# An adaLN block with attention and a router of two experts: the weight search by quarters of the partitions, and four moves at its edges

## The chip, the cores and the metric

One NeuronCore of a Trainium2 chip runs the whole kernel; the metric is the device time in microseconds of that core. The engines are TensorE (PE, matmul, with PEld for its weight loads), VectorE (DVE), ScalarE (ACT), GpSimd (POOL) and SyncE (SP, which here only issues transfers).

## The reference, cut to what matters

Input `x` is 8 batches of 256 tokens by 128 features.

```
mod = silu(c) @ wmod -> sa, ca, ga, sb, cb, gb      (ga, gb kept at least 0.25 in size)
h = layernorm(x) * (1 + ca) + sa
x = x + ga * attention(h)       16 heads of 8, ALiBi slopes, causal softmax, W_o
h = layernorm(x) * (1 + cb) + sb
x = x + gb * ffn(h)
ffn: probs = softmax(layernorm(h) * gamma + beta) @ Wr + br over 8 experts
     y_e = gelu(h @ W1_e + b1_e) @ W2_e + b2_e;   out = sum_e probs_e * y_e
     expert 0 has the weights as given; experts 1 to 7 all share one altered copy:
     thr_bot, thr_top = the 3276th smallest and the 3276th largest |w| of the matrix
     w -> 0.2 w where |w| >= thr_top;   1.8 w where |w| <= thr_bot
```

b1 and b2 are altered likewise. So only two experts are computed, plain and altered, the second with the sum of seven probabilities. For W1 and W2 (65,536 numbers each) the two thresholds have to be found exactly.

## The kernel before, in words

**The search.** The four thresholds (top and bottom of W1 and of W2) are found bit by bit, 31 bits, each from a count of how many |w| lie below a candidate. W1's absolute values lie in `wa` on partitions 0 to 63 and W2's on 64 to 127, 1,024 columns each. The candidate tile `cand` has a column for the top threshold and one for the bottom, so each bit needs two passes over `wa`: `sign_count(n, TOP, 1024)` on ACT, then `sign_count(n, BOT, 512)` on ACT beside `dve_counts(n)` (L1203, the other 512 columns) on DVE. In the five steps of `BY_ACT` ACT takes all 1,024 columns of both. `total(n)` (L936, L938) sums over partitions with two tiny matmuls into `psX`, `decide(n)` (L1208) compares, `next_cand(n)` (L1214) sets the next candidate. Bits 0 and 1 come ahead of the main loop, then one a step in steps 0 to 30 but 23 and 27.

**The loop.** Each engine has its program written out by hand; semaphores alone tie them. Steps t = 0 to 39: each of the first 32 takes four heads of one batch through scores (`s_unit`, L767 first), row maxima (`maxima`, L1224, L1228, DVE), with a lag of five steps the exponentials (`e_unit`, `exp_unit`, L578), the causal cut on POOL (L491), the product with the values (`pv`, L820), transposes and division. Four steps make a batch. Queries and keys are split in bf16 parts by `high_parts`, `remainder` and `lower_parts` (for batch 0 by `first_parts` and `first_split`), written to DRAM (L297 to L307) and read back in stacked order by `stack(b)` (L322): batch 0 in two groups of heads, on which step 0 (18.14 us) and step 1 (22.68 us) wait. `max_rows` (L328) copies the maxima, 16 KB from 32 partitions to 2.

**Start.** SP issues all input transfers in one queue, in the order of L262 to L276: `x[0]`, `c`, the first part of `wmod`, `x[1]`, `w_o`, the two of `wa` (L267, L268, 256 KB each, 64 partitions of 4 KB), the rest of `wmod`, the constant rows, `x[2]`, small vectors. Behind them in the same queue come the writes of the parts and `stack(0)`. ACT waits for `wa` (L640) before `first_parts`, DVE likewise (L1391) before `first_split`.

**After the loop**, for four pairs of batches, PE runs `f1` (L903, weights 1) and `f2` (L923, weights 2) for plain and altered weights, `c_pe_h` (L859, transposes) and `c_pe_l` (L866, L870, router sums of h and of its squares). DVE runs `router_moments`, `router_logits`, `router_weights` (L1287 to L1301), `squares` (L1258) and `combine` (L1316 to L1331); POOL the exponential of the logits (`c_exp`, L461) and the second normalisations (`second_normal`, L449), batch b's in step 12 + 4b (one later from batch 5 on).

Of the kernel before, what the change touches and what calls it, by code (L numbers as in the profile page):

```python
# [16 lines left out]
F32 = mybir.dt.float32  # L17
# [14 lines left out]
G = 4  # L32
# [26 lines left out]
NORM2_AT = {AT_Y + G * b + 1 + (b >= LATE): b for b in range(B - 1)}  # L59
# [16 lines left out]
HALF_SETS = 17  # L76
HALF = P // 2
ON_ACT = FF
TOP, BOT = 0, 1
SIGNED_ALL = 2 * (K_STAT - 1) - P * FF  # L80
SIGNED_TOP = 2 * (P * FF - K_STAT) - P * FF
SIGNED_BOT = 2 * (K_STAT - 1) - HALF * ON_ACT


def adaln_block(nc, x, w_qkv, w_o, w1, b1, w2, b2, gamma, beta, wr, br, c, wmod,
                k_const, q_const, ident_c, parts_dram, rows_dram, thr_dram, out):
    with ExitStack() as ctx:
# [11 lines left out]
        halves = sb("halves", [P, 2, P], F16)  # L99
# [8 lines left out]
        wa = sb("wa", [P, 2 * FF])  # L108
# [88 lines left out]
        bits_x = psX[:, B1_COLS - 8:B1_COLS - 6].bitcast(U32)  # L197
# [22 lines left out]
        b_scratch = msk[:, 2:4].rearrange("p a f -> p (a f)")  # L220
        d_scratch = b_scratch[:, ON_ACT:2 * FF]
        psF = (psS[0], psS[1], psQ, psE[0])
        assert len(psF) == NF
        block = ctx.enter_context(nc.Block())
# [28 lines left out]
        def _(sp):  # L253
# [13 lines left out]
            sp.dma_start(wa[0:HALF, :], w1.rearrange("(p r) f -> p (r f)", r=2)).then_inc(q["wa_in"], 16)  # L267
            sp.dma_start(wa[HALF:P, :], w2.rearrange("(p r) d -> p (r d)", r=8)).then_inc(q["wa_in"], 16)  # L268
# [105 lines left out]
            for k in range(2):  # L374
                sp.wait_ge(q["ob_done"], NPAIR + k)
                sp.dma_start(out[B - 2 + k].rearrange("(i t) d -> t i d", t=P),
                             ob[:, (NPAIR - 1) % 2, NBLK * k:NBLK * (k + 1)]).then_inc(stored[(NPAIR - 1) % 2], 16)
            sp.wait_ge(stored[0], 16 * 2)
            sp.wait_ge(stored[1], 16 * 3)
# [3 lines left out]
        def _(gp):  # L383
# [97 lines left out]
            for t in range(T_END):  # L481
# [28 lines left out]
                if t == FFN_STEP:  # L510
                    c_exp(0)
            second_rstd(B - 1)
# [8 lines left out]
        def _(act):  # L521
# [64 lines left out]
            def sign_count(n, col, width):  # L586
# [5 lines left out]
                scratch = msk[:, 0:2].rearrange("p a f -> p (a f)") if col == TOP else b_scratch[:, 0:width]  # L592
                with nc.allow_low_precision(reason="sums of up to 1024 signs are integers that float16 holds"):
                    act.activation(scratch, wa[:, 0:width], ACT.Sign, bias=cand[:, col:col + 1].bitcast(F32),  # L594
                                   scale=-(1.0 - 2.0 ** -24), accum_out=acc[:, col:col + 1]).then_inc(q["m_act"], 1)
# [55 lines left out]

            for t in range(T_END):
# [4 lines left out]
                if n is not None:  # L657
                    sign_count(n, TOP, 2 * FF)
                    sign_count(n, BOT, 2 * FF if n in BY_ACT else ON_ACT)
# [49 lines left out]
        def _(pe):  # L709
# [195 lines left out]
            def f2(n):  # L905
# [641 lines left out]
```

## Time and profile before

| what | value |
|---|---|
| three runs, us | 227.58, 228.4, 232.05 (median 228.4) |
| the profiled execution's own time | 229.65 us |
| its span, first to last instruction | 227.9 us, mean granted TensorE clock 0.989 |
| busy, share of the span | PE 91%, DVE 76%, ACT 72%, PEld 62%, POOL 57% |
| transfers on SP's queue | 19.23 MB, 32.2% of the 16 DMA engines' span |
| main loop | step 0 at 18.14 us, step 31 at 142.34 us; a batch takes 16.3 to 16.5 us in the middle |

Busy shares are means over stages with different limits, so each part of the change is read from the stage in which it lies. The chain of waits is the path followed back from the last instruction to what released it each time. "Idle before" is the idle time of the engine ahead of an instruction, with what ended it. The DMA share is the mean busy share of 16 DMA engines; packets overlap, so it can pass 1.

### The profile page before, as it was taken

Reading aid. Unit: us, or ns where it says so; the run is one execution under the profiler, and the core shown is the slowest. Engines: PE = TensorE matmul, PEld = TensorE weight load, DVE = VectorE, ACT = ScalarE, POOL = GpSimd, SP = SyncE. Lnnn points to the kernel's source line nnn. Section 1 sums busy time; section 2 is a strip of 40 time slices with the busy share of each in tenths; the row PEclk is TensorE's granted clock in tenths of the full one; section 3 lists DMA queues with packets and bytes.
Section 4 is the critical chain, followed back from the end, with each engine's and each line's share of the span. In section 5 each row is a group of like instructions: output and inputs, shape, how many; then the busy total and the mean of one; then the engine's idle time right before and its main releaser. Section 6 shows DMA issues by size and latency. Waiting matters only on the chain.

```text
span 227.9 us, 5343 instructions
## 1 busy us (share of the span) xinstructions
PE 208.2 (91%) x1876; PEld 140.4 (62%) x1876; DVE 174.3 (76%) x534; ACT 163.6 (72%) x348; POOL 131.0 (57%) x211
## 2 busy tenths in 40 slices
PE   7686979999999999999998999998999979999993
PEld 3343646566576575666655666655677974786792
DVE  5675779998899899898889799769679493373465
ACT  2489678999999999999799799667759303344310
POOL 6852331765878867864764364379699826504600
PEclk9999999999999999999999999999999997999998
DMA  5848583984947046055238100000000010010011
GB/s 165 145 150 253 136 211 90 217 218 110 223 138 190 9 116 188 0 161 145 73 97 204 30 6 0 0 7 0 3 1 3 0 46 3 0 46 0 3 46 47
DMA packets 19350, 19.84 MB, mean 87 GB/s; under 512 B 1436, under 2 KB 17459, under 8 KB 18259
## 3 DMA queue, kind: packets, MB, share of 16 engines
q1 hardware_dynamic: 18778, 19.23, 32.2%
q8 instruction: 15, 0.25, 0.5%
q10 hardware_dynamic: 544, 0.26, 0.4%
q14 instruction: 13, 0.10, 0.2%
HBM read 14.11 MB, written 5.25 MB: 85 GB/s over the span
## 4 chain that ended last, share of the span: by engine, by line
PE 53%; ACT 15%; DVE 13%; issue 7%; DMA 6%; POOL 2%; SPq 2%; ACTq 0%; DVEq 0%
PE bank L923 11%; PE bank L903 10%; ACT msk L594 8%; PE bank L820 5%; ACT PT L578 4%; PE bank L799 3%; DMA Ks<-parts 3%; PE bank L777 3%; PE bank L886 2%; DMA wa<-in_w 2%; PE bank L773 2%; DVE nmax L1228 2%; PE bank L825 2%; PE bank L958 2%; PE bank L838 2%
## 5 line engine op out<-in xcount | busy, mean ns | idle before, releaser
L491 POOL TENSOR_SCALAR_AFFINE_SELECT PT<-PT 128x256 f32<-128x256 f32 (+1 forms) x96 | 47.6, 506 | 38.7 <-ACT PT L578 35.6
L594 ACT ACTIVATE msk<-wa,cand 128x1024 bf16<-128x1024 f32 (+1 forms) x62 | 60.4, 996 | 3.7 <-DVE cand L1214 3.6
L578 ACT ACTIVATE PT<-bank 128x512 f32<-128x512 f32 x96 | 55.1, 620 | 3.0 <-PE bank L794 2.2
L1228 DVE TENSOR_REDUCE nmax<-bank 128x2 f32<-128x512 f32 x64 | 43.6, 686 | 3.0 <-PE bank L777 2.3
L799 PE MATMUL bank<-Qs,Ks 80*128 80x256 bf16 x128 | 24.7, 274 | 1.8 <-ACT PT L578 1.3
L1224 DVE TENSOR_REDUCE nmax<-bank 128x4 f32<-128x512 f32 x32 | 21.7, 679 | 5.8 <-PE bank L770 5.8
L777 PE MATMUL bank<-Ks,Qs 78*128 78x256 bf16 x128 | 24.4, 272 | 0.0
L461 POOL TENSOR_TENSOR ex<-eul,lg 128x32 f32<-128x32 f32 x4 | 21.7, 5436 | 2.7 <-DVE lg L1283 2.7
L1316 DVE SCALAR_TENSOR_TENSOR yt<-bank,pr,yt 128x128 f32<-128x128 f32 x32 | 9.1, 345 | 17.2 <-PE bank L923 17.1
L820 PE MATMUL bank<-PT,Vx 128*32 128x256 f32 x256 | 20.4, 390 | 1.2 <-POOL PT L491 0.6
L773 PE MATMUL bank<-mask 128*128 128x256 bf16 x64 | 17.7, 276 | 2.9 <-DVE nmax L1228 2.1
L1203 DVE TENSOR_SCALAR_CACHE_REDUCE msk<-wa,cand 128x512 bf16<-128x512 f32 x26 | 19.4, 745 | 0.9
L695 ACT ACTIVATE U<-bank 128x256 f32<-128x256 f32 x32 | 12.9, 405 | 6.5 <-PE bank L825 6.2
L623 ACT ACTIVATE hid<-bank,b1p 128x512 f32<-128x512 f32 x16 | 10.7, 688 | 9.1 <-PE bank L903 9.0
L623 ACT ACTIVATE hid<-bank,cols 128x512 f32<-128x512 f32 x8 | 5.5, 687 | 14.6 <-PE bank L903 14.6
L923 PEld LDWEIGHTS bank<-w2p,hid 128*128 128x128 f32 x128 | 14.8, 192 | 1.4 <-issue 1.4
L716 PE MATMUL bank<-ones_b 128*128 128x512 bf16 x49 | 14.6, 412 | 1.0 <-POOL ones_b L384 1.0
L903 PE MATMUL bank<-h2T,w1p 128*128 128x512 f32 x32 | 15.1, 598 | 0.0
L923 PE MATMUL bank<-w2p,hid 128*128 128x128 f32 x128 | 14.9, 275 | 0.0
L767 PE MATMUL bank<-mask 128*128 128x512 bf16 x32 | 12.1, 379 | 2.3 <-DMA Ks<-parts 1.8
L455 POOL TENSOR_TENSOR rs<-ve,mhalf 128x4 f32<-128x4 f32 x4 | 4.3, 1068 | 17.2 <-DVE ve L1271 17.2
L594 ACT ACTIVATION_READ_ACCUMULATOR msk<-wa,cand 128x1 f16 x62 | 14.1, 228 | 0.0
(210 smaller groups left out, 468.3 us busy)
## 6 DMA issues: line engine op xcount, KB each, us to landing
Qs<-parts SPq DMA_DIRECT2D x7, 576.0 KB
Ks<-parts SPq DMA_DIRECT2D x7, 576.0 KB
parts<-part SPq DMA_DIRECT2D x7, 384.0 KB, 3.0
x_all<-in_x SPq DMA_DIRECT2D x8, 128.0 KB, 7.0
parts<-part SPq DMA_DIRECT2D x8, 128.0 KB, 2.9
rows_bc<-rows_out SPq DMA_DIRECT2D x2, 512.0 KB, 10.0
out<-ob SPq DMA_DIRECT2D x3, 256.0 KB, 2.3
wa<-in_w SPq DMA_DIRECT2D x2, 256.0 KB, 4.6
```

Of the source, the lines that this page charges most:

```text
L461: gp.tensor_tensor(ex[:, :, :], eul[:, :, :], lg2[:, p % 2], op=ALU.pow).then_inc(q["ex_done"], 1)
L491: gp.affine_select(out=v, in_=v, compare_op=ALU.is_ge, fill=0.0, base=0, pattern=[[0, v.shape[1]], [1, P]], channel_multiplier=-1).then_in ...
L578: act.activation(PT[:, e % 2, j], psE[u % 2][:, :], ACT.Exp).then_inc(q["exp_done"], 1)
L594: act.activation(scratch, wa[:, 0:width], ACT.Sign, bias=cand[:, col:col + 1].bitcast(F32), scale=-(1.0 - 2.0 ** -24), accum_out=acc[:, co ...
L773: mm(bank.rearrange("p (h k) -> p h k", h=2)[:, :, P:S], mask5[:, HG, :], mask5[:, 0:2, :], start=True, stop=False, skip_group_check=True)
L777: last = mm(bank[:, i * S:(i + 1) * S], Qs[0:R_S, r, h, P:S], Ks[0:R_S, r, h, :], start=False, stop=True, skip_group_check=True)
L799: last = mm(bank[:, i * S:(i + 1) * S], Ks[0:R_E, r, h, 0:P], Qs[0:R_E, r, h, :], start=True, stop=True, skip_group_check=True)
L820: mm(psO[32 * i:32 * i + 32, 0:S], Vx[:, b % 4, 0, h, :], PT[:, e % 2, 1 + i // 2, (i % 2) * S:(i % 2 + 1) * S], start=True, stop=False, s ...
L903: mm(psF[ch][:, :], wt[:, ch * P:(ch + 1) * P], h2T[:, p % 2], start=True, stop=True).then_inc(q["f1_done"], 1)
L923: last = mm(bank[:, i * P:(i + 1) * P], hid_of(n)[:, ch, i * P:(i + 1) * P], wt[:, ch, :], start=(ch == 0), stop=(ch == NC - 1), skip_grou ...
L1224: ve.tensor_reduce(nmax[:, b % 2, 0, HG * g:HG * (g + 1)], bank.rearrange("p (h k) -> p h k", h=HG), axis=AX.X, op=ALU.max, negate=True).t ...
L1228: ve.tensor_reduce(nmax[:, b % 2, 1, h:h + 2], bank.rearrange("p (h k) -> p h k", h=2), axis=AX.X, op=ALU.max, negate=True).then_inc(q["ma ...
```

## The change

Five parts.

1. **Search by quarters.** `wa` gets 2,048 columns: W1 on partitions 0 to 31 and once more on 32 to 63, W2 on 64 to 95 and 96 to 127. The first quarter of each matrix holds the candidate for the top, the second that for the bottom, so `cand` has one column and a bit needs one sign: 1,536 columns on ACT with 512 on DVE (2,048 on ACT in `BY_ACT`). Each of the two transfers of `wa` now reads its matrix twice, through a source pattern of 2 repeats by 32 rows by 2,048 columns into 64 partitions: 512 KB each. The sums use `quarters`, the limits lie in a tile, the thresholds leave in one transfer.
2. **Start order.** `first_parts`, `value_copy(0)` and `first_split` come ahead of the wait for `wa`; on PE batch 1's transposes and projections come ahead of the late `wmod` matmuls and of `total(0)`.
3. **Last normalisations later.** Batches 5 and 6 are normalised on POOL after the loop, ahead of batch 7's.
4. **Squares ahead of the router's weights** on DVE.
5. **Last sums in two operations.** `combine` multiplies by `gb` and adds `x` after the plain expert, so that after the altered one only a product of three and a sum are left; the last pair's altered half is stored in pieces of 2, 1 and 1 blocks instead of 2 and 2.

```diff
@@ -73,13 +73,10 @@
 NPAIR = B // 2
 BY_ACT = [n for n, t in enumerate(SLOT) if 0 <= t < E_LAG]
 POOL_SETS = 10
-HALF_SETS = 17
-HALF = P // 2
-ON_ACT = FF
-TOP, BOT = 0, 1
-SIGNED_ALL = 2 * (K_STAT - 1) - P * FF
-SIGNED_TOP = 2 * (P * FF - K_STAT) - P * FF
-SIGNED_BOT = 2 * (K_STAT - 1) - HALF * ON_ACT
+HALF_SETS = 1 + 8 + 8
+QUART = P // 4
+ON_ACT = 3 * FF
+TOP_LIMIT, BOT_LIMIT = 2 * (P * FF - K_STAT), 2 * (K_STAT - 1)
 
 
 def adaln_block(nc, x, w_qkv, w_o, w1, b1, w2, b2, gamma, beta, wr, br, c, wmod,
...
             sp.dma_start(wo_in[:, :], w_o).then_inc(q["wo_in"], 16)
-            sp.dma_start(wa[0:HALF, :], w1.rearrange("(p r) f -> p (r f)", r=2)).then_inc(q["wa_in"], 16)
-            sp.dma_start(wa[HALF:P, :], w2.rearrange("(p r) d -> p (r d)", r=8)).then_inc(q["wa_in"], 16)
+            for w, weights in enumerate((w1, w2)):
+                twice = bass.AP(tensor=weights.tensor, offset=weights.offset, ap=[[0, 2], [4 * FF, QUART], [1, 4 * FF]])
+                sp.dma_start(wa[2 * QUART * w:2 * QUART * (w + 1), :], twice).then_inc(q["wa_in"], 16)
             sp.dma_start(wmod_sb[:, 2 * D:6 * D], wmod[:, 2 * D:6 * D]).then_inc(q["modrow_in"], 16)
             fixed_rows(0)
             block_in(2)
...
                 sp.wait_ge(q["cand_done"], NBITS + 1)
-                sp.dma_start(thr_dram[0:1, :], cur[0:1, :]).then_inc(q["thr_out"], 16)
-                sp.dma_start(thr_dram[1:2, :], cur[HALF:HALF + 1, :]).then_inc(q["thr_out"], 16)
-                sp.wait_ge(q["thr_out"], 32)
+                sp.dma_start(thr_dram.rearrange("a b -> (a b)").unsqueeze(1), cur[0:P:QUART, :]).then_inc(q["thr_out"], 16)
+                sp.wait_ge(q["thr_out"], 16)
...
+            second_normal(B - 3)
+            second_normal(B - 2)
             second_rstd(B - 1)
             second_normal(B - 1)
             for p in range(1, NPAIR):
...
 
-            def sign_count(n, col, width):
+            def sign_count(n):
                 if n == 0:
                     act.wait_ge(q["wa_dve"], 1)
                 act.wait_ge(q["cand_done"], n + 1)
-                    act.activation(scratch, wa[:, 0:width], ACT.Sign, bias=cand[:, col:col + 1].bitcast(F32),
-                                   scale=-(1.0 - 2.0 ** -24), accum_out=acc[:, col:col + 1]).then_inc(q["m_act"], 1)
+                width = 4 * FF if n in BY_ACT else ON_ACT
+                with nc.allow_low_precision(reason="sums of up to 2048 signs are integers that float16 holds"):
...
             scaled(0)
+            first_parts()
+            value_copy(0)
             act.wait_ge(q["wa_in"], 32)
             act.activation(wa[:, 0:FF], wa[:, 0:FF], ACT.Abs).then_inc(q["wa_act"], 1)
-            first_parts()
+            scaled(1)
             act.wait_ge(q["wa_act"], 1)
-            sign_count(0, TOP, 2 * FF)
-            value_copy(0)
-            sign_count(0, BOT, ON_ACT)
-            scaled(1)
-            sign_count(1, TOP, 2 * FF)
+            sign_count(0)
             high_parts(1)
-            sign_count(1, BOT, ON_ACT)
+            sign_count(1)
 
             for t in range(T_END):
                 n = sel_bit(t)
...
             values(0)
+            turned(1)
+            projected(1)
+            spare(2)
             pe.wait_ge(q["modrow_in"], 16)
             mm(psE[1][0:B, 0:512], c_s[:, :], wmod_sb[:, 2 * D:6 * D], start=True, stop=True).then_inc(q["pe_set"], 1)
             pe.wait_ge(q["dve_set"], SETS["modT"])
             for j in range(2):
                 last = mm(psE[0][:, j * B:(j + 1) * B], wmod_sb[:, (3 + j) * D:(4 + j) * D], c_s[:, :], start=True, stop=True)
             last.then_inc(q["pe_set"], 1)
-            turned(1)
             total(0)
-            projected(1)
-            spare(4)
             vectors()
+            spare(2)
+            values(1)
             total(1)
-            values(1)
 
             for t in range(T_END):
                 n = sel_bit(t)
...
                 p, w = n // 2, n % 2
+                xp = x_all[:, 2 * p:2 * p + 2].rearrange("p b i d -> p (b i) d")
                 if w == 0:
-                    pieces = ((psO, range(4)),)
-                elif p < NPAIR - 1:
-                    pieces = ((psU, range(4)),)
-                else:
-                    pieces = ((psU, range(2)), (psX, range(2, 4)))
-                for k, (bank, blocks) in enumerate(pieces):
-                    bs = slice(blocks[0], blocks[-1] + 1)
+                    v.wait_ge(q["f2_done"], n + 1)
+                    for i in range(4):
+                        last = ve.scalar_tensor_tensor(yt[:, 0, i], psO[:, i * P:(i + 1) * P], pr[:, p % 2, 0, i:i + 1],
+                                                       yt[:, 1, i], op0=ALU.mult, op1=ALU.add)
+                    last.then_inc(q["y_read"], 1)
+                    v.wait_ge(q["y_read"], n + 1)
+                    if p == 0:
+                        v.wait_ge(q["gb_in"], 16)
+                    for k in range(2):
+                        last = ve.tensor_tensor(yt[:, 0, NBLK * k:NBLK * (k + 1)], yt[:, 0, NBLK * k:NBLK * (k + 1)],
+                                                rows_bc[:, 2 * p + k, 1, :].unsqueeze(1).broadcast_to([P, NBLK, D]), op=ALU.mult)
+                    then_self(last)
+                    then_self(ve.tensor_tensor(yt[:, 0], yt[:, 0], xp, op=ALU.add))
+                    return
+                for k, (bank, blocks) in enumerate(LAST_PIECES if p == NPAIR - 1 else ((psU, range(4)),)):
                     v.wait_ge(q["f2_done"], n + 1 + k)
                     for i in blocks:
-                        last = ve.scalar_tensor_tensor(yt[:, w, i], bank[:, i * P:(i + 1) * P], pr[:, p % 2, w, i:i + 1],
-                                                       yt[:, 1 - w, i], op0=ALU.mult, op1=ALU.add)
+                        last = ve.scalar_tensor_tensor(yt[:, 1, i], bank[:, i * P:(i + 1) * P], pr[:, p % 2, 1, i:i + 1],
+                                                       rows_bc[:, 2 * p + i // NBLK, 1, :], op0=ALU.mult, op1=ALU.mult)
                     last.then_inc(q["y_read"], 1)
+                    if p >= 2 and k == 0:
+                        v.wait_ge(stored[p % 2], 16 * (p // 2))
                     v.wait_ge(q["y_read"], n + 1 + k)
-                    if w:
-                        for i in blocks[::NBLK]:
-                            b = 2 * p + i // NBLK
-                            last = ve.tensor_tensor(yt[:, 1, i:i + NBLK], yt[:, 1, i:i + NBLK],
-                                                    rows_bc[:, b, 1, :].unsqueeze(1).broadcast_to([P, NBLK, D]), op=ALU.mult)
-                        if p == 0 and k == 0:
-                            v.wait_ge(q["gb_in"], 16)
-                        if p >= 2 and k == 0:
-                            v.wait_ge(stored[p % 2], 16 * (p // 2))
-                        then_self(last)
-                        xp = x_all[:, 2 * p:2 * p + 2].rearrange("p b i d -> p (b i) d")
-                        ve.tensor_tensor(ob[:, p % 2, bs], yt[:, 1, bs], xp[:, bs], op=ALU.add).then_inc(q["ob_done"], 1)
+                    bs = slice(blocks[0], blocks[-1] + 1)
+                    ve.tensor_tensor(ob[:, p % 2, bs], yt[:, 1, bs], yt[:, 0, bs], op=ALU.add).then_inc(q["ob_done"], 1)
 
             def find_tiers(ready, w, a, top, bot):
 
...
 
+            first_split()
             v.wait_ge(q["wa_in"], 32)
-            absolute(wa[:, FF:2 * FF], wa[:, FF:2 * FF]).then_inc(q["wa_dve"], 1)
-            first_split()
+            absolute(wa[:, FF:4 * FF], wa[:, FF:4 * FF]).then_inc(q["wa_dve"], 1)
             v.wait_ge(q["wa_dve"], 1)
             dve_counts(0)
             v.wait_ge(q["pe_set"], 4)
                 elif p < NPAIR:
-                    router_weights(p)
                     if p + 1 < NPAIR:
                         squares(p + 1)
+                    router_weights(p)
 
 
```

Left out of it: tile shapes, `half_sums` replaced by `quarter_sums` (17 small memsets each), `NORM2_AT` over `range(B - 3)`, the third piece in `f2`, in `LAST_PIECES` and in the last stores, and `total`, `decide` and `dve_counts` with one column (the first matmul of `total` goes in `BY_ACT`).

## Rows read from the trace of the kernel before

**Rows 1.** The page: shares of the span on the chain of waits, by engine and line

```profile
PE bank L923 11%; PE bank L903 10%; ACT msk L594 8%; PE bank L820 5%; ACT PT L578 4%; PE bank L799 3%; DMA Ks<-parts 3%; PE bank L777 3%; PE bank L886 2%; DMA wa<-in_w 2%; PE bank L773 2%; DVE nmax L1228 2%; PE bank L825 2%; PE bank L958 2%; PE bank L838 2%
```

**Rows 2.** Busy time by stretch: us, busy us of each engine, clock, DMA share, GB/s

```profile
86.79:103.07 16.28, 15.53 (x182) 10.24 (x178) 15.17 (x42) 15.96 (x38) 11.81 (x24) 1.00 0.38 106
```

**Rows 3.** The chain of waits up to the second step: start, us, what

```profile
3.76 5.12 DMA wa<-in_w
...
8.91 0.63 ACT wa L641
...
16.09 6.54 DMA Ks<-parts
```

**Rows 4.** Timeline of the start: start, us, engine, line, operation, [idle before]

```profile
7.16 1.13 PE L958 MATMUL bank<-h1T,wqkT 128*128 128x256 f32 x4 [0.44 <-ACT h1T L535]
...
11.20 0.38 SPq L297 DMA_DIRECT2D parts<-part  x1
...
13.21 0.18 PE L938 MATMUL bank<-acc,halves 128*128 128x2 f16 x1
...
13.33 0.91 SPq L322 DMA_DIRECT2D Qs<-parts  x1
...
16.38 0.18 PE L938 MATMUL bank<-acc,halves 128*128 128x2 f16 x1 [0.27 <-ACT msk L594]
...
18.14 0.38 PE L767 MATMUL bank<-mask 128*128 128x512 bf16 x1 [1.03 <-DMA Ks<-parts]
```

**Rows 5.** As rows 2: the first transfers; writing parts; stacking; the maxima's rows

```profile
2.00:5.00 3.00, 3.00 (x11) 1.02 (x9) 1.79 (x16) 1.18 (x2) 1.96 (x6) 1.00 0.85 232
81.00:82.00 1.00, 1.00 (x15) 0.67 (x13) 0.93 (x4) 1.00 (x4) 0.43 (x2) 1.00 0.93 289
86.50:89.50 3.00, 2.85 (x32) 1.77 (x25) 2.90 (x8) 3.00 (x8) 2.01 (x5) 1.00 0.76 202
133.25:133.50 0.25, 0.25 (x5) 0.19 (x3) 0.21 (x2) 0.25 (x2) 0.24 (x1) 1.00 0.14 39
```

**Rows 6.** ScalarE's timeline over one bit of the search

```profile
51.90 1.16 ACT L594 ACTIVATE msk<-wa,cand 128x1024 bf16<-128x1024 f32 x1
...
53.03 0.73 ACT L594 ACTIVATE msk<-wa,cand 128x512 bf16<-128x512 f32 x1
...
53.73 0.57 ACT L535 ACTIVATE h1T<-bank,modT 128x256 f32<-128x256 f32 x1
```

**Rows 7.** Timeline around the sixth second normalisation

```profile
153.42 1.81 POOL L449 TENSOR_SCALAR n<-x_all,mv,rs 128x128 f32<-128x128 f32 x2
...
157.32 0.64 PE L820 MATMUL bank<-PT,Vx 128*32 128x256 f32 x8 [0.63 <-POOL PT L491]
```

**Rows 8.** Timeline of the feed-forward stage and the end

```profile
186.62 0.69 DVE L1258 TENSOR_TENSOR sq<-h2T 128x512 f32<-128x512 f32 x1
...
187.36 1.05 PE L870 MATMUL bank<-wrg,sq 128*128 128x1 f32 x8 [1.46 <-DVE sq L1258]
...
188.28 5.38 PE L903 MATMUL bank<-h2T,w_sb 128*128 128x512 f32 x8
...
206.21 3.68 PE L903 MATMUL bank<-h2T,w_sb 128*128 128x512 f32 x8
...
209.25 5.43 POOL L461 TENSOR_TENSOR ex<-eul,lg 128x32 f32<-128x32 f32 x1 [1.04 <-DVE lg L1283]
...
214.66 0.76 DVE L1323 TENSOR_TENSOR yt<-yt,rows_bc 128x256 f32<-128x256 f32 x2
...
215.53 0.69 DVE L1331 TENSOR_TENSOR ob<-yt,x_all 128x512 f32<-128x512 f32 x1
...
220.31 3.74 PE L923 MATMUL bank<-w2p,hid 128*128 128x128 f32 x32
...
225.19 0.42 DVE L1331 TENSOR_TENSOR ob<-yt,x_all 128x256 f32<-128x256 f32 x1
```

**Rows 9.** The same columns as rows 2, for three us of that stage

```profile
189.00:192.00 3.00, 3.00 (x5) 1.32 (x4) 1.02 (x6) 0.91 (x2) 1.70 (x2) 0.50 0.00 0
```

More of the change, by code:

```diff
@@ L58 @@
 RSTD2_AT = {AT_Y + G * b + (b >= LATE): b for b in range(B - 1)}
-NORM2_AT = {AT_Y + G * b + 1 + (b >= LATE): b for b in range(B - 1)}
+NORM2_AT = {AT_Y + G * b + 1 + (b >= LATE): b for b in range(B - 3)}
 MOMENT_STEP, SQUARE_STEP = 37, 34
@@ L372, in _ @@
                 sp.dma_start(out[2 * p:2 * p + 2].rearrange("b (i t) d -> t (b i) d", t=P), ob[:, p % 2]).then_inc(stored[p % 2], 16)
-            for k in range(2):
+            for k, (_, blocks) in enumerate(LAST_PIECES):
+                b, i = B - 2 + blocks[0] // NBLK, blocks[0] % NBLK
                 sp.wait_ge(q["ob_done"], NPAIR + k)
-                sp.dma_start(out[B - 2 + k].rearrange("(i t) d -> t i d", t=P),
-                             ob[:, (NPAIR - 1) % 2, NBLK * k:NBLK * (k + 1)]).then_inc(stored[(NPAIR - 1) % 2], 16)
+                sp.dma_start(out[b, i * P:(i + len(blocks)) * P].rearrange("(i t) d -> t i d", t=P),
+                             ob[:, (NPAIR - 1) % 2, blocks[0]:blocks[-1] + 1]).then_inc(stored[(NPAIR - 1) % 2], 16)
             sp.wait_ge(stored[0], 16 * 2)
-            sp.wait_ge(stored[1], 16 * 3)
+            sp.wait_ge(stored[1], 16 * (1 + len(LAST_PIECES)))
         @block.gpsimd
@@ L591, in sign_count @@
                     act.wait_ge(q["tot_done"], n)
-                scratch = msk[:, 0:2].rearrange("p a f -> p (a f)") if col == TOP else b_scratch[:, 0:width]
-                with nc.allow_low_precision(reason="sums of up to 1024 signs are integers that float16 holds"):
-                    act.activation(scratch, wa[:, 0:width], ACT.Sign, bias=cand[:, col:col + 1].bitcast(F32),
-                                   scale=-(1.0 - 2.0 ** -24), accum_out=acc[:, col:col + 1]).then_inc(q["m_act"], 1)
+                width = 4 * FF if n in BY_ACT else ON_ACT
+                with nc.allow_low_precision(reason="sums of up to 2048 signs are integers that float16 holds"):
+                    act.activation(scratch[:, 0:width], wa[:, 0:width], ACT.Sign, bias=cand[:, 0:1].bitcast(F32),
+                                   scale=-(1.0 - 2.0 ** -24), accum_out=acc[:, :]).then_inc(q["m_act"], 1)
             def c_act_h(p):
@@ L930, in total @@
                     return
-                if n not in BY_ACT:
-                    pe.wait_ge(q["m_dve"], sum(k not in BY_ACT for k in range(n + 1)))
                 if n == 0:
@@ L935, in total @@
                 claim_x((q["cand_done"], n + 2))
-                mm(psX[:, 0:2], halves[:, 1, :], (acc_z if n in BY_ACT else acc_d)[:, :], start=True, stop=False)
-                pe.wait_ge(q["m_act"], 2 * (n + 1))
-                mm(psX[:, 0:2], halves[:, 0, :], acc[:, :], start=False, stop=True).then_inc(q["tot_done"], 1)
+                if n not in BY_ACT:
+                    pe.wait_ge(q["m_dve"], sum(k not in BY_ACT for k in range(n + 1)))
+                    mm(psX[:, 0:1], quarters[:, 1, :], acc_d[:, :], start=True, stop=False)
+                pe.wait_ge(q["m_act"], n + 1)
+                mm(psX[:, 0:1], quarters[:, 0, :], acc[:, :], start=n in BY_ACT, stop=True).then_inc(q["tot_done"], 1)
             def turned(b):
@@ L1201, in dve_counts @@
                 v.wait_ge(q["cand_done"], n + 1)
-                with nc.allow_low_precision(reason="counts of up to 1024 are integers that float16 holds"):
-                    ve.tensor_scalar(d_scratch, wa[:, ON_ACT:2 * FF], cand[:, BOT:BOT + 1].bitcast(F32), 0.0, op0=ALU.is_le,
-                                     op1=ALU.add, accum_out=acc_d[:, BOT:BOT + 1]).then_inc(q["m_dve"], 1)
+                with nc.allow_low_precision(reason="counts of up to 512 are integers that float16 holds"):
+                    ve.tensor_scalar(scratch[:, ON_ACT:4 * FF], wa[:, ON_ACT:4 * FF], cand[:, 0:1].bitcast(F32), 0.0, op0=ALU.is_le,
+                                     op1=ALU.add, accum_out=acc_d[:, :]).then_inc(q["m_dve"], 1)
             def decide(n):
                 v.wait_ge(q["tot_done"], n + 1)
-                ve.tensor_scalar(bits_x, psX[:, 0:2], float(SIGNED_ALL if n in BY_ACT else SIGNED_BOT), float(1 << (NBITS - 1 - n)), op0=ALU.is_le,
+                if n == 0:
+                    v.wait_ge(q["half_set"], HALF_SETS)
+                way = 1 if n in BY_ACT else 0
+                ve.tensor_scalar(bits_x, psX[:, 0:1], limit[:, way:way + 1], float(1 << (NBITS - 1 - n)), op0=ALU.is_le,
                                  op1=ALU.mult).then_inc(q["cond_done"], 1)
```

57 lines of the change are left out of this document (27 added, 30 removed).

## The prediction

> **What bounds the kernel now.** I read the shares of the chain of waits first, then busy times by stretch, then the timeline where each part of the change lies. The chain [rows 1] belongs to no single engine: TensorE's two feed-forward lines have 21% of the span, ScalarE's signs (L594) 8%. In the middle of the loop ScalarE is busiest, 15.96 of 16.28 us for a batch, but VectorE has 15.17 and TensorE 15.53 [rows 2], so relief for ScalarE alone is soon used up. At the start the chain runs through transfers: `wa` lands at 8.88, and step 1 begins when the last of the stacked parts lands at 22.63 [rows 3]. Most of what follows hangs on that start.
>
> **The start: `wa` from two DMA engines.** Both transfers of `wa` get a source pattern whose outermost count is 2, and 64 partitions on the other side. What the outermost counts do can be read from three kinds of transfer, each alone in its stretch [rows 5]. Parts written from 128 partitions run at a share of 0.93 and 289 GB/s. The stacked reads (24 source rows outermost, 72 partitions) sit at 0.76 and 202 GB/s: 12 of 16 engines, and 12 is the largest number up to 16 that divides both 24 and 72. The maxima's rows (32 partitions into 2) reach 0.14 and 39 GB/s: two of 16. One pattern fits all three: the transfer is split over the largest number of engines, up to 16, that divides the outermost count of both sides. For counts 2 and 64 that is two engines. Before, `wa` had 64 against 64, so 16.
>
> The price. An engine moves 202 / 12 = 16.8 GB/s in the stacked reads and 39 / 2 = 19.5 in the maxima's rows. The two transfers are 1,049 KB, now 524 KB on each of two engines: 26.9 to 31.2 us. The stacked reads are nearer (DRAM to SBUF, long rows), but twelve engines load the memory more than two do; I take 29. Ahead of `wa` in the queues are 0.7 MB at 232 GB/s from 2.0 us on [rows 5], so its part begins at about 5.0 and ends at 34.0, where `wa` landed at 8.88 before [rows 3].
>
> What is queued behind it: the two engines carry a sixteenth each of the late `wmod` (16 KB), whole constant rows (8 + 8 KB), `x[2]` (8 KB) and a sixteenth of the query parts (12 KB), 52 KB or 3 us more. So the query parts, issued at 11.20 and landed at 13.33 before [rows 4], land at 37, 23.7 us later. `stack(0)` is issued behind them by SP, and steps 0 and 1 wait for it: 24 us later, between +21.3 and +26.0 by the two rates.
>
> This doesn't rest on the queue alone. `total(0)` and `total(1)` stand ahead of the loop on TensorE, and the second of them came 7.5 us after `wa` landed (16.38 against 8.88) [rows 3, 4]. From 34.0 that is 41.5, against 18.14 for step 0 before: 23.4 us. Taking `first_parts` and `first_split` out from behind `wa` would free them by 1.7 us (the projections end at 8.3, the absolute values at 9.54 [rows 3, 4]); behind two full engines it buys nothing. The other moves of the start (batch 1's projections forward, four `spare` matmuls in two pairs) lie in the same wait, and VectorE's longer absolute values add under a microsecond inside the 7.5.
>
> The Trainium skill, "DMA: Bandwidth & Descriptors", section "Why a DMA increments its semaphore by 16 and not by 1", gives the same split: an engine count that divides the outermost dimension of both sides. The trace agrees in the three transfers above. Its section "Where 436 GB/s comes from" puts the fabric at 435 GB/s for 16 engines; at 27 GB/s an engine `wa` would take 19.3 us, an estimate from that page, and my sum would be some 237 instead of 246.5. No row here shows an engine that fast.
>
> **Clock.** TensorE has next to nothing to do from about 14 to 34 us. After a pause of 1.46 us behind small matmuls the granted clock was 0.50, the 1.2 GHz level [rows 8, 9], and the four f1 chunks took 5.38 us where another time they took 3.68. I expect the half clock when `wa` lands. Projections, `wmod` and totals then take up to 2 us more; step 1's transfers cover most of it. I take 0.5, ends 0 and 2. The skill's "TensorE: Matmul & The Clock Gate", section "What's actually happening", also has an idle TensorE fall to 1.2 GHz; with no such fall my sum is 0.5 lower.
>
> **The search in the loop.** On ScalarE 1,024 columns take 1.13 us from start to start and 512 take 0.70 [rows 6], the accumulator read within. That is 0.84 ns a column, so 1,536 take 1.56, and a bit falls from 1.83 to 1.56: 0.27 us, 8 us over 31 bits. The signs' 8% of the span [rows 1] is 18.2 us, ten bits' worth, so no more than 2.7 us can leave the end. VectorE, whose 512-column count stays, and TensorE are near [rows 2]; I take 2.3, ends 0.5 and 2.7. One tiny matmul less in `BY_ACT`, one column instead of two in `decide` and `next_cand`, and the limit from a tile: nothing, they lie between waits. The threshold's single transfer lands far ahead of its first use: nothing.
>
> **Last normalisations.** The sixth takes POOL 1.81 us at 153.42, and the product with the values then waits 0.63 for POOL [rows 7]: 0.6 comes back, 0 if another operand is late. Later, the two cost POOL 3.6 us behind the first exponential's 5.4 [rows 8], 9 us in all; TensorE needs batch 5 only after three blocks of 3.6, 10.8 us: hidden, and a delay of up to 1 us if POOL starts late.
>
> **Squares first.** TensorE waits 1.46 us for the squares of pair 2 (L1258, begun at 186.62) [rows 8]. Ahead of the router's weights they start some 2.8 us earlier, three operations of 0.69 and small ones; the wait goes whole, and with it the half clock behind it: 5.38 - 3.68 = 1.7 us. Together 3.2. If the clock falls anyway, 1.5.
>
> What is late next: the plain `combine` grows by 0.76 + 0.69 = 1.45 us [rows 8] ahead of the next logits, and the weights of a pair now stand behind squares that wait for TensorE's transposes. Before, the last exponential began at 209.25 and took 5.43, and f2's last block began at 220.31 [rows 8]. Moved up by 3.2 these are 206.05 and 217.1. Weights take 2.8. So the exponential may be 217.1 - 2.8 - 5.43 - 206.05 = 2.8 us late at no cost; I expect 1.8. Past 2.8, each microsecond costs one.
>
> **Last sums.** The piece behind the last matmul has one block, product and sum, where it had two blocks, product, gate and sum. But VectorE is then still on the plain half, longer by 1.45. By order of its work the end comes about as long after the last matmul as before; the smaller store gives 0.2, ends 0 and 0.9 (two operations of 0.42 and one block of product [rows 8]). Two more operations a pair elsewhere lie beside TensorE.
>
> **The sum**, against the profiled execution's 229.65 us: + 24.0 start + 0.5 clock - 2.3 search - 0.6 normalisations - 3.2 squares - 0.2 end = 247.85. That execution stood 1.25 us above the median of 228.4; against the median, 246.6. I say 246.5. With all bounds at their ends it would be 242 to 256; errors don't all fall one way, so 243 to 252.
>
> **Rivals.**
>
> *`wa` is spread over 16 engines all the same* (0.15). For it: the pattern is read off three transfers, of which only the maxima's has a 2, and there on the destination. Against: in each of them the smaller or common divisor ruled, whichever side it was on. Then the extra 524 KB cost 2.2 us at 232 GB/s; the parts are ready 1.7 us earlier but queue behind it: +0.9 net. With the other terms 224.3, against the median 223.0: the other side, faster by 2.4%. It decides at `wa`'s landing: below about 14 us.
>
> *Two engines, but the queue behind isn't held* (0.10, within the forecast's side). Then TensorE's order sets the start by the 7.5 us above: +23.4 at step 0, less at step 1, since its transfers are there: 245.
>
> *Something between* (0.03): four to eight engines, `wa` at 12 to 19 us, 226 to 234.
>
> **How the numbers follow.** The forecast has 0.72; with the second rival two engines have 0.82, all of it over 238. The range 238 to 254 takes in both rates, the clock and engines that are somewhat faster alone; outside lie 0.15, 0.03 and a little above. A measurement of this kernel tells about 2% from no change, 223.8 to 233.0. Faster by over 2%: two thirds of the spread case, 0.10. Within: the rest of it and half of the third, 0.06. Slower: 0.84.
>
> **What would show it.** Two engines: `wa` lands at 30 to 37 us, the DMA share stays near 0.12 and 33 to 39 GB/s from about 9 us until then, step 0 begins at 40 to 45. A share near 1 and a landing near 11 would prove me wrong. Search: one sign of 1,536 columns at 1.5 to 1.6 us, batches of 15.8 to 16.2 us. Squares: no wait ahead of L870 in pair 2, its f1 chunks in 3.7 us at full clock. End: the last sum about 1.5 us behind the last matmul.

## The result and the profile after

The changed kernel takes 248.6 us (median of 6 runs, 247.6 to 253.27) where the kernel before takes 228.66 beside it (227.58 to 232.05): a ratio of 1.0837, 95% interval 1.0788 to 1.0886. Predicted were 246.5 us and slower. The execution that was profiled took 253.27 us (span 251.5), 4.7 above the median, in a slower state that two of the six runs show, so its start may read some microseconds too long; where that matters the runs below are used.

The chain of waits of the changed kernel up to the first projection (start, us, what), against [rows 3]:

```profile
3.87 32.56 DMA wa<-in_w
36.45 0.97 DVE wa L1107
...
37.59 2.08 PE bank L955 x4
```

The same columns as [rows 5], for two stretches inside that transfer:

```profile
14.00:20.00 6.00, 0.00 (x0) 0.00 (x0) 0.00 (x0) 0.00 (x0) 0.00 (x0) 0.50 0.13 30
20.00:26.00 6.00, 0.00 (x0) 0.00 (x0) 0.00 (x0) 0.00 (x0) 0.00 (x0) 0.50 0.14 33
```

`wa` landed at 36.43 instead of 8.88. From about 12 us until then no engine computes; in these stretches the DMA share is 0.13 (two engines of 16 are 0.125), the rate 30 to 33 GB/s, and the granted clock 0.50. The four projections then take 2.08 us; before they took 1.13 [rows 4]. SP's queue in the meantime:

```profile
6.77 7.69 SPq L270 DMA_DIRECT2D vecs<-in_b  x1
14.50 3.21 SPq L272 DMA_DIRECT2D vecs<-in_b  x1
...
22.84 3.35 SPq L295 DMA_DIRECT2D parts<-part  x1
26.23 8.27 SPq L297 DMA_DIRECT2D parts<-part  x1
34.55 0.49 SPq L298 DMA_DIRECT2D parts<-part  x1
```

Issues that took 0.25 to 0.52 us before take up to 8.27 us: what is queued waits, and so does SP itself. The stacking's first read is issued at 39.34 instead of 13.33, and step 0 starts at 45.60 instead of 18.14:

```profile
45.58 0.16 PE L935 MATMUL bank<-acc,quarters 128*128 128x1 f16 x1
45.60 0.38 PE L764 MATMUL bank<-mask 128*128 128x512 bf16 x1
```

The total of the second bit stands directly ahead of step 0 on TensorE. Where the rest of the time is, in four positions of the trace (us):

| kernel | first score product | first product behind the loop | last f2 matmul | span |
|---|---|---|---|---|
| before | 18.4 | 170.3 | 223.8 | 227.9 |
| changed | 45.8 | 197.5 | 247.7 | 251.5 |
| difference | +27.4 | +27.2 | +23.9 | +23.6 |
| e4 (below) | 41.8 | 191.7 | 241.9 | 245.7 |
| difference to before | +23.4 | +21.4 | +18.1 | +17.8 |

e4 differs from the changed kernel only in the queue that issues `wa`, and its profiled execution took 247.46 us. From the first score product to the end of the loop the changed kernel gains 0.2 us on the kernel before in this trace, e4 1.9. In the first steps the granted clock of the changed kernel was still low (0.61 from 45 to 50 us, 0.71 from 50 to 55), that of e4 was 1.00 from 40 us on.

The second feed-forward pair, against [rows 8]:

```profile
210.14 0.69 DVE L1255 TENSOR_TENSOR sq<-h2T 128x512 f32<-128x512 f32 x1
...
212.99 1.03 PE L867 MATMUL bank<-wrg,sq 128*128 128x1 f32 x8
213.88 3.68 PE L900 MATMUL bank<-h2T,w_sb 128*128 128x512 f32 x8
```

The squares are ready 2.2 us ahead of their sums, no wait is left, and the chunks take 3.68 us: 3.3 us come back here. At the end of the loop GpSimd still holds TensorE up, for 0.76 us, and the last piece ends 1.5 us behind the last matmul, as before:

```profile
187.37 0.64 PE L817 MATMUL bank<-PT,Vx 128*32 128x256 f32 x8 [0.76 <-POOL PT L489]
...
244.22 3.74 PE L920 MATMUL bank<-w2p,hid 128*128 128x128 f32 x32
...
249.20 0.29 DVE L1329 TENSOR_TENSOR ob<-yt 128x128 f32<-128x128 f32 x1
```

### The profile page after: what moved, and what is told of

Read it like the earlier page. It is cut to its first block, busy times and chain, and to the rows that moved or that the text cites. A ratio compares the mean times of both kernels' runs of the same rounds, so it can differ in the third digit from the quotient of the medians.

```text
span 251.5 us, 5253 instructions
## 1 busy us (share of the span) xinstructions
PE 207.8 (83%) x1871; PEld 142.1 (57%) x1871; DVE 178.9 (71%) x539; ACT 157.7 (63%) x286; POOL 130.8 (52%) x211
## 4 chain that ended last, share of the span: by engine, by line
PE 57%; DVE 17%; DMA 13%; ACT 5%; issue 4%; SPq 1%; POOL 1%; DVEq 0%; ACTq 0%
DMA wa<-in_w 13%; PE bank L920 10%; PE bank L900 8%; PE bank L817 6%; DVE nmax L1225 4%; PE bank L774 3%; PE bank L955 3%; PE bank L883 3%; PE bank L796 3%; DVE msk L1197 3%; PE bank L770 3%; PE bank L713 2%; ACT msk L594 2%; PE bank L822 2%; PE bank L835 2%
## 5 line engine op out<-in xcount | busy, mean ns | idle before, releaser
L578 ACT ACTIVATE PT<-bank 128x512 f32<-128x512 f32 x96 | 54.5, 604 | 3.6 <-PE bank L791 2.5
L594 ACT ACTIVATE msk<-wa,cand 128x1536 bf16<-128x1536 f32 (+1 forms) x31 | 51.3, 1655 | 7.7 <-DVE cand L1211 7.7
L955 PE MATMUL bank<-h1T,wqkT 128*128 128x256 f32 x32 | 9.4, 420 | 26.3 <-ACT h1T L535 26.3
L796 PE MATMUL bank<-Qs,Ks 80*128 80x256 bf16 x128 | 24.5, 273 | 0.9 <-ACT PT L578 0.9
L955 PEld LDWEIGHTS bank<-h1T,wqkT 128*128 128x128 f32 x32 | 6.0, 207 | 27.6 <-ACT h1T L535 26.9
L395 POOL TENSOR_SCALAR ve<-mv 128x2 f32<-128x2 f32 x7 | 1.6, 236 | 37.3 <-DVE mv L1115 37.2
L1107 DVE TENSOR_SCALAR wa<-wa 128x1536 uint32<-128x1536 uint32 x1 | 1.0, 960 | 26.4 <-DMA wa<-in_w 26.4
L713 PE MATMUL bank<-ones_b 128*128 128x512 bf16 x49 | 17.3, 470 | 1.0 <-POOL ones_b L382 1.0
L643 ACT ACTIVATE wa<-wa 128x512 f32<-128x512 f32 x1 | 0.6, 632 | 26.1 <-DMA wa<-in_w 26.1
```

The costliest lines, as they stand in the source:

```text
L578: act.activation(PT[:, e % 2, j], psE[u % 2][:, :], ACT.Exp).then_inc(q["exp_done"], 1)
L594: act.activation(scratch[:, 0:width], wa[:, 0:width], ACT.Sign, bias=cand[:, 0:1].bitcast(F32), scale=-(1.0 - 2.0 ** -24), accum_out=acc[: ...
L796: last = mm(bank[:, i * S:(i + 1) * S], Ks[0:R_E, r, h, 0:P], Qs[0:R_E, r, h, :], start=True, stop=True, skip_group_check=True)
L955: last = mm(bank, wqkT[:, a, :], h1T[:, b % 2], start=True, stop=True)
```

## The experiments

Theory A: the outermost count of 2 in `wa`'s source leaves the transfer to two engines. Theory B: the doubled bytes cost the time. Twelve runs in three sets (e1 to e4, e5 to e8, e9 to e12), each set on one chip; the kernel before took 229.61, 230.09 and 229.91 us there. "The base" is the kernel of e1, the changed one without its slow load. Some expectations call `wa` the router's matrix, the parts of queries and keys partial products, and the batches tiles.

**e1: the changed kernel, `wa` in four transfers of 32 rows.**

```diff
-            for w, weights in enumerate((w1, w2)):
-                twice = bass.AP(..., ap=[[0, 2], [4 * FF, QUART], [1, 4 * FF]])
-                sp.dma_start(wa[2 * QUART * w:2 * QUART * (w + 1), :], twice)...
+            for w, weights in enumerate((w1, w2)):
+                for copy in range(2):
+                    lo = QUART * (2 * w + copy)
+                    once = bass.AP(..., ap=[[4 * FF, QUART], [1, 4 * FF]])
+                    sp.dma_start(wa[lo:lo + QUART, :], once)...
```

> The changed kernel, with wa loaded by four transfers of 32 rows of 8 KB, one for each quarter, in place of two with a source pattern of 2 repeats by 32 rows; the bytes and everything else stay. Theory A (the outermost count of 2 puts wa on two DMA engines): wa lands near 11 us in place of 36, step 0 begins at 18 to 20, and the time is 222 to 225. Theory B (the doubled bytes cost the time, whatever the engines): wa still lands at 30 or later and the time stays at 247 to 249.

226.79 us, ratio 0.9889 [0.9845, 0.9934]. Its timeline:

```profile
11.66 0.96 DVE L1109 TENSOR_SCALAR wa<-wa 128x1536 uint32<-128x1536 uint32 x1 [0.32 <-DMA wa<-in_w]
...
16.22 0.92 SPq L322 DMA_DIRECT2D Qs<-parts  x1
...
21.53 0.63 PE L769 MATMUL bank<-Ks,Qs 78*128 78x128 bf16 x4 [2.80 <-ACT msk L596]
```

The same bytes and the same search, without the count of 2: the loss is gone. So A, and B is out as the cause, though the time is 2 us above the 222 to 225 that A gave. What stays is a start 3.1 us later (21.5 against 18.4). The wait ahead of step 0 is put down to a sign of ScalarE, but step 0 doesn't need that one (in e12 it starts before it). It is rather the stacked reads, whose first is issued at 16.22 instead of 13.33, as in e11, where the same wait is put down to the reads.

**e2: source patterns with 4 outermost.**

```diff
-                    once = bass.AP(..., ap=[[4 * FF, QUART], [1, 4 * FF]])
+                    once = bass.AP(..., ap=[[4 * FF, 4], [16 * FF, 8], [1, 4 * FF]])
```

> As the run with sixteen engines, but each of the four source patterns has 4 outermost by 8 rows (the rows permuted within the quarter). Theory A: four engines with 262 KB each, 16 us at 16.5 GB/s an engine, wa lands at 20 to 22, the DMA share stays near 0.25 until then, and the time is 231 to 235. Theory B: no difference from the run with sixteen engines.

234.78 us, ratio 1.0236 [1.0155, 1.0317], as theory A gave; `wa` is there at 18.4, somewhat before the 20 to 22 expected:

```profile
18.43 0.96 DVE L1109 TENSOR_SCALAR wa<-wa 128x1536 uint32<-128x1536 uint32 x1 [7.08 <-DMA wa<-in_w]
```

**e3: the kernel before, its `wa` in its own bytes, 2 outermost.**

```diff
-            sp.dma_start(wa[0:HALF, :], w1.rearrange("(p r) f -> p (r f)", r=2))...
-            sp.dma_start(wa[HALF:P, :], w2.rearrange("(p r) d -> p (r d)", r=8))...
+            for w, weights in enumerate((w1, w2)):
+                swapped = bass.AP(..., ap=[[2 * FF, 2], [4 * FF, HALF // 2], [1, 2 * FF]])
+                sp.dma_start(wa[HALF * w:HALF * (w + 1), :], swapped)...
```

The rows of `wa` come in another order, which changes no count of the search.

> The kernel before with only the source patterns of wa's two transfers changed: 2 outermost by 32 rows of 4 KB (rows permuted, bytes as before, 256 KB each). Theory A: two engines with 262 KB each, wa lands at 20 to 22, all that is queued behind follows, and the time is 239 to 243. Theory B (doubled bytes): nothing is doubled here, the time stays at 228 to 229.

240.7 us, ratio 1.0521 [1.044, 1.0602], as theory A gave. The load is there at 17.55 instead of 8.91, again before the 20 to 22 expected:

```profile
17.55 0.43 DVE L1110 TENSOR_SCALAR wa<-wa 128x512 uint32<-128x512 uint32 x1 [10.09 <-DMA wa<-in_w]
```

The order of the counts alone, on the kernel before, costs 5%. From issue to landing one engine moved 524 KB in 32.56 us (changed kernel), 16.1 GB/s, and in 29.28 us (e4), 17.9; 262 KB in 13.69 us (e3), 19.1, and in 13.11 us (e2, four engines), 20.0. That time holds what was ahead and beside in the queues too, so the engines themselves can be faster. Stretches in which about two engines are busy show their rate (columns as [rows 5]; the changed kernel, e3, e4):

```profile
9.00:26.00 17.00, 1.34 (x8) 0.72 (x6) 0.98 (x3) 0.95 (x3) 2.05 (x4) 0.59 0.13 31
```

```profile
9.00:17.00 8.00, 0.27 (x2) 0.00 (x0) 0.00 (x0) 0.00 (x0) 1.80 (x4) 0.85 0.14 54
```

```profile
20.00:26.00 6.00, 1.64 (x7) 1.05 (x6) 0.00 (x0) 0.38 (x1) 0.00 (x0) 0.78 0.13 51
```

Halved, these are 15.5, 27 and 25.5 GB/s an engine. Why the changed kernel's profiled execution was slower here isn't known.

**e4: the changed kernel, its two transfers issued by ScalarE's queue.**

```diff
-                sp.dma_start(wa[2 * QUART * w:2 * QUART * (w + 1), :], twice)...
+                act.dma_start(wa[2 * QUART * w:2 * QUART * (w + 1), :], twice)...
```

> The changed kernel with wa's two transfers, patterns as they are, issued by ScalarE on its own queue behind the attention weights. Theory A1 (TensorE's order: two totals of the search stand ahead of the loop): wa still lands at 30 to 36, batch 0's parts land near 13, step 0 begins some 7.5 us behind wa and the time falls by 0 to 3 us only, 245 to 249. Theory A2 (what costs is SP's queue held up behind wa): step 0 begins near 20 and the time is 225 to 232.

250.16 us, ratio 1.0942 [1.0829, 1.1055]: nothing won. `wa` is there at 32.27, the stacking's reads are issued from 32.81 (39.34 in the changed kernel), and the first score product still comes 9.5 us behind `wa`:

```profile
32.27 0.96 DVE L1107 TENSOR_SCALAR wa<-wa 128x1536 uint32<-128x1536 uint32 x1 [15.03 <-DMA wa<-in_w]
...
41.53 0.16 PE L935 MATMUL bank<-acc,quarters 128*128 128x1 f16 x1
41.77 0.39 PE L767 MATMUL bank<-Ks,Qs 78*128 78x128 bf16 x4
```

The reads are issued 0.5 us behind `wa`'s landing, where they came 2.9 behind it in the changed kernel, and step 0 follows `wa` at the same distance (9.5 and 9.4 us), right behind the second total. So the order on TensorE, `total(0)` and `total(1)` ahead of step 0, is enough to hold the start. But e4 doesn't free SP's queue: one of its issues is held for 8.96 us (last section), and the reads still come at 32.81, not near 13.

**e5: the base, squares behind the router's weights again.**

```diff
-                    if p + 1 < NPAIR:
-                        squares(p + 1)
                     router_weights(p)
+                    if p + 1 < NPAIR:
+                        squares(p + 1)
```

> This kernel is the changed one with its router matrix from sixteen engines (four transfers of 32 rows, as in the run that came to 226.8 us on another chip), but the squares of the second pair are again behind the router's weights. The prediction's term: the 1.46 us wait ahead of the squares' sums and the 1.7 us that the half clock takes of the first layer come back, so 3.2 us above the sixteen-engine kernel: 230 us where that is 226.8. Rival: the clock falls anyway or the wait is only moved; then 1.5 us or nothing above it. The trace should show a wait of over 1 us ahead of the squares' sums of the second pair and first-layer chunks of about 5.4 us instead of 3.7 in one place.

232.84 us, ratio 1.0131 [1.0067, 1.0195], against 0.992 and 0.9889 of the base: 2.1 to 2.4%, some 5 us, more than the 3.2 expected. Its timeline shows why:

```profile
180.66 5.44 POOL L461 TENSOR_TENSOR ex<-eul,lg 128x32 f32<-128x32 f32 x1
...
188.98 0.69 DVE L1257 TENSOR_TENSOR sq<-h2T 128x512 f32<-128x512 f32 x1
189.73 1.05 PE L869 MATMUL bank<-wrg,sq 128*128 128x1 f32 x8 [3.47 <-DVE sq L1257]
190.64 5.38 PE L902 MATMUL bank<-h2T,w_sb 128*128 128x512 f32 x8
```

The wait is 3.47 us, not 1.46 [rows 8]: the exponential begins 10.0 us after the loop (180.66 against 170.6) where it began 7.9 after it before (178.15 against 170.3). VectorE's router weights wait for it, and squares behind them wait too. With 3.47 - 1.46 = 2.0 us more, and 3.2, the trace gives 5.2. Two parts of the change delay the exponential, and e7 and e6 below have one of them each. With the late normalisations alone ahead of it on GpSimd it begins 9.9 us after the loop (e7, first line; 182.47 against 172.5), with the longer plain `combine` alone ahead of the logits on VectorE 9.4 (e6, second line; 179.97 against 170.6):

```profile
182.47 5.45 POOL L460 TENSOR_TENSOR ex<-eul,lg 128x32 f32<-128x32 f32 x1
```

```profile
179.97 5.45 POOL L461 TENSOR_TENSOR ex<-eul,lg 128x32 f32<-128x32 f32 x1 [2.13 <-DVE lg L1280]
```

The edits aren't independent: squares first also hides what these two cost.

**e6: the base, normalisations 5 and 6 in the loop again.**

```diff
-NORM2_AT = {AT_Y + G * b + 1 + (b >= LATE): b for b in range(B - 3)}
+NORM2_AT = {AT_Y + G * b + 1 + (b >= LATE): b for b in range(B - 1)}
...
-            second_normal(B - 3)
-            second_normal(B - 2)
```

> The sixteen-engine kernel with the second normalisations of tiles 5 and 6 back inside the attention loop. The prediction's term: 0.6 us more, 227.4 where that kernel is 226.8. Rival, from the trace of the changed kernel, where TensorE still waits 0.76 us on GpSimd's last mask ahead of the last values product: the move bought nothing, and the two kernels are the same within 0.3 us.

226.47 us, ratio 0.9888 [0.9851, 0.9925]: as the base, as the rival gave. The wait for GpSimd is in another place. First e6, then the base:

```profile
157.62 0.64 PE L817 MATMUL bank<-PT,Vx 128*32 128x256 f32 x8 [0.64 <-POOL PT L491]
...
160.44 0.64 PE L817 MATMUL bank<-PT,Vx 128*32 128x256 f32 x8
```

```profile
158.44 0.64 PE L819 MATMUL bank<-PT,Vx 128*32 128x256 f32 x8
161.88 0.64 PE L819 MATMUL bank<-PT,Vx 128*32 128x256 f32 x8 [0.76 <-POOL PT L491]
```

**e7: the base, last sums as before** (`combine`, the pieces of f2 and the two last stores of the kernel before).

```diff
-            for k, (_, blocks) in enumerate(LAST_PIECES):
+            for k in range(2):
...
-                        bank = LAST_PIECES[i - 1][0]
+                        bank = psX
```

> The sixteen-engine kernel with the sums behind the second layer as before the change. The prediction's term: 0.2 us more (0 to 0.9). The tail behind the last matmul was 1.56 us in the kernel before and 1.53 in the changed one, so by the traces nothing, within 0.3 us.

226.78 us, ratio 0.9894 [0.985, 0.9938]: as the base. From the start of the last f2 matmul to the end of the span it is 4.3 us here (222.7 to 227.0), 3.8 in the base (222.2 to 226.0) and 4.1 in the kernel before: 0.3 to 0.5 us by the trace, less than these runs tell apart.

**e8: the kernel before, squares first, nothing else** (the diff of e5 the other way).

> The kernel before, with one thing of the change: the squares of the second pair are ahead of the router's weights. No change of the search and of the router matrix's load. The prediction's term alone: 3.2 us off (the 1.46 us wait and 1.7 us of half clock), 225.5 where the kernel before is 228.7, ratio 0.986. Rival: with the clock falling elsewhere only 1.5 us off, ratio 0.993; and if the wait moves behind another operation, nothing.

227.04 us, ratio 0.9922 [0.9882, 0.9961]. The span is 224.7, 3.2 below the 227.9 of the kernel before, all of it in one place, where that kernel had the wait and the half clock [rows 8]:

```profile
185.83 1.03 PE L870 MATMUL bank<-wrg,sq 128*128 128x1 f32 x8
186.73 3.68 PE L903 MATMUL bank<-h2T,w_sb 128*128 128x512 f32 x8
```

Wait and half clock both go, and the trace shows no new fall of the clock behind the loop. The medians differ by 3.05 us; the runs' interval holds 0.9 to 2.7 us, which is less than the 3.2 and would fit the rival's 1.5 too. It is the trace that decides between them.

**e9 and e10: can the 3.1 us at the base's start be had back?** e9 issues the four transfers from ScalarE's queue, e10 puts `fixed_rows(0)` and `block_in(2)` ahead of them.

```diff
-                    sp.dma_start(wa[lo:lo + QUART, :], once)...
+                    act.dma_start(wa[lo:lo + QUART, :], once)...
```

```diff
+            fixed_rows(0)
+            block_in(2)
             for w, weights in enumerate((w1, w2)):
...
-            fixed_rows(0)
-            block_in(2)
```

> The sixteen-engine kernel with the router matrix's four transfers issued by ScalarE's queue instead of SyncE's. In the sixteen-engine kernel step 0 of the attention starts 3.1 us later than in the kernel before (21.5 against 18.4), since its partial products are written 5.4 us after their issue instead of 2.1, behind 1 MB of the matrix in the rings of one queue. If that order within the queue is what costs (theory Q), the other queue takes some 2 us off the start: 224.5 to 225 where the sixteen-engine kernel is 226.8. If it is the bytes themselves that all engines share (theory B), nothing is won: 226 to 228.

> The sixteen-engine kernel with the third tile of x and the constant rows of the first step issued ahead of the router matrix. The third tile then lands at about 12 us instead of 15.45. If the later tiles' late landing is what delays the steps behind step 0 (steps 1 and 2 start 4 us later than in the kernel before), this gives up to 1.5 us: 225.3. If step 0's partial products set the start, nothing changes: 226.8 within 0.5 us.

228.3 us (0.9984 [0.9939, 1.003]) and 228.66 us (0.9965 [0.9924, 1.0006]), against 226.76 of the base: 1.5 to 1.9 us worse by the medians, and the intervals just overlap the base's. The third batch of `x` landed early (its statistics at 10.31 and 7.37 instead of 15.48), and step 0 follows the second total. First e9, then e10:

```profile
13.96 0.95 DVE L1109 TENSOR_SCALAR wa<-wa 128x1536 uint32<-128x1536 uint32 x1
...
22.62 0.17 PE L937 MATMUL bank<-acc,quarters 128*128 128x1 f16 x1
22.65 0.59 PE L766 MATMUL bank<-mask 128*128 128x512 bf16 x1
```

```profile
14.13 0.96 DVE L1109 TENSOR_SCALAR wa<-wa 128x1536 uint32<-128x1536 uint32 x1 [3.97 <-DMA wa<-in_w]
...
22.25 0.16 PE L937 MATMUL bank<-acc,quarters 128*128 128x1 f16 x1
22.27 0.38 PE L766 MATMUL bank<-mask 128*128 128x512 bf16 x1
```

Theory Q falls: e9 is even a little above what theory B gave, and e10 is outside both of its expectations. What holds the start isn't the same in the three. In e10 `wa` lands later (14.11 against 11.6) and the second total comes 8.1 us behind it. In e9 nothing waits for `wa`: the chain goes back to the first part of `wmod`, and batch 0's projections begin at 10.18, at half clock (2.07 us). In the base the two paths are of nearly equal length. In e1 step 0 comes 2.5 us behind the second total (18.57), which is the wait for the stacked reads, in e12, the same kernel, right behind it:

```profile
20.65 0.17 PE L937 MATMUL bank<-acc,quarters 128*128 128x1 f16 x1
20.68 0.59 PE L766 MATMUL bank<-mask 128*128 128x512 bf16 x1
```

So neither move could win much alone, and which share of the late start is the bytes' stays open.

**e11: the search by quarters** (e1's load; squares, normalisations and sums as before). The expectation says "alone", but the changed order of the start stays in.

> The kernel before with the search by quarters of the partitions alone, its router matrix from sixteen engines; squares, normalisations and last sums as before. The prediction's search term (2.3 us off) and the 3.1 us by which twice the bytes delay step 0 leave it 0.8 us above the kernel before, ratio 1.003, if the wait ahead of the squares' sums stays at 1.46 us. Rival, from the run without the squares first: there that wait was 3.47 us and the run came to 1.3% above the kernel before; then this one does too, ratio 1.01.

230.56 us, ratio 1.0025 [0.9974, 1.0076]: as expected, no change. The wait ahead of the squares' sums is again 1.46 us. So the quarters don't make the 3.47 of e5; it comes from the late normalisations and the longer `combine`:

```profile
187.84 1.05 PE L866 MATMUL bank<-wrg,sq 128*128 128x1 f32 x8 [1.46 <-DVE sq L1254]
```

Its first score product is 2.1 us later than before (20.5), behind a wait of 1.98 us for the stacked reads, and the loop from there on is 1.6 us shorter (150.3 against 151.9). What the order of the start brings by itself was not tried.

**e12: the base again.**

> The sixteen-engine kernel again, as the base of the three others on their chip: 226.8 us, ratio 0.989 to the kernel before.

226.76 us, ratio 0.992 [0.987, 0.9969]. Base and e8 are about 1% faster than the kernel before and can't be told from each other.

## Why the prediction was right

The mechanism was right, and the total is 2.1 us off. In e4's trace the three stretches are +23.4 at the start (predicted with the clock 24.5), -1.9 in the loop (-2.9) and -3.6 behind it (-3.4).

- **Start, 24.0 predicted.** In the profiled execution +27.4; by the medians the two engines cost 248.6 - 226.8 = 21.8 us, and with sixteen engines the doubled bytes leave a start 2.1 to 3.1 later (e11, e1): 24 to 25. Mechanism shown by e1, e2 and e3. The 29 us from 5.0 on stand for 18.1 GB/s an engine; reckoned in the same way the landings give 16.7 (changed kernel) and 19.2 (e4). That this mean came out is in part luck: in the stretches above an engine moved between 15.5 and 27 GB/s. The prediction says that no row shows an engine at 27; e3 does, for 8 us, and its load still took 13.69 us.
- **What holds step 0.** Predicted were two things of equal length, the queue and TensorE's order. In e4 the reads come 2.4 us earlier behind `wa` and step 0 doesn't: the order suffices. That the queue alone would do it too wasn't tried. From `wa` to the second total it was 9.1 us (e4 9.3), not the 7.5 of before.
- **Clock, 0.5.** The mechanism was right, the size too small: at 0.50 the projections alone take 0.95 us more (2.08 against 1.13), and the path behind `wa` is 1.6 to 1.8 us longer than the 7.5, near the upper end given. The two `wmod` matmuls behind them, on the chain too, take 1.88 us instead of 1.02. How much of the 1.6 to 1.8 is clock and how much the other order of the start was not separated.
- **Search, 2.3.** Over-sized. A sign of 1,536 columns takes 1.58 us, as predicted (1.56), and the loop gets 1.6 us shorter (e11), within the ends of 0.5 and 2.7. That more of the signs lies off the chain than was taken is likely, but not shown. With the doubled load paid, quarters bring nothing (e11, 1.0025).
- **Normalisations, 0.6.** Wrong: the wait moved by one product with the values, from 0.64 to 0.76 us (e6). And "hidden" held only by the squares' new place; without it the move and the longer `combine` together cost 2.0 us (e5).
- **Squares, 3.2.** 3.2 in the span of e8, 3.3 in the changed kernel, by the traces; the runs of e8 give 0.9 to 2.7.
- **What is late next.** The last exponential was expected 1.8 us late with 2.8 to spare: it begins 9.05 us ahead of the last f2 block instead of 11.06 [rows 8], 2.0 late, at no cost.
- **Last sums, 0.2.** 0.3 to 0.5 by the traces, nothing in the runs (e7).
- **Two figures of the working.** The ends as given add up to 255.4 at the top, not 256. The parts were said to be free 1.7 us earlier, but the two times beside it, 8.3 and 9.54, differ by 1.2; in the base their writing is issued at 9.81 (e12) instead of 11.20, 1.4 earlier.

The rival of 16 engines decided where it was said to, at `wa`'s landing. Where it is made true (e1, `wa` there at 11.7) the time is 226.8, not the 223.0 worked out for it: the start costs 3.1 us (e12: 2.7) where 0.9 was expected, and search and normalisations together bring 1.5 where 2.9 was.

## What to carry to other kernels

The copy made here by a zero-stride dimension was the outermost count of the source, and that count set over how many DMA engines the transfer was spread (2, 4 and 16 were tried): write such a load as one transfer for each copy. A wait taken off one engine is only worth what the engine behind it doesn't spend next, so an edit that "moves work to where it is hidden" has to be costed together with the edit that hides it. At the start of a kernel, follow the first load that an in-order engine's early work depends on, not only the loads that the main loop reads.

## What the runs showed of the hardware

- While two DMA engines worked off `wa` in the changed kernel, SP was held at its issues: 3.2 to 8.3 us for some that took 0.25 to 0.5 us before. In e4, where `wa` was in ScalarE's queue, one of SP's issues was still held for 8.96 us:

```profile
18.44 8.96 SPq L295 DMA_DIRECT2D parts<-part  x1
```

- With about two DMA engines busy, an engine moved 15.5 GB/s in the changed kernel's profile, 25.5 in e4's and 27 in e3's, against 16.8 in the stacked reads on twelve [rows 5]. Over the whole load, from issue to landing, it was 16 to 20.
- Four engines cost 8 us against sixteen (234.8 against 226.8), two cost 22; `wa` is there at 18.4 and 36.4 (32.3 in e4) against 11.7.
